# Grouped mixture of experts: the first five blocks run while rows are still being placed, and the shared units stand between the one-hot products

## The reference

```python
E, I, K = 64, 176, 6                                   # experts, width, chosen per token
probs = softmax(x @ gate_w.T)
topk_w, topk_idx = top_k(probs, K)
topk_w = topk_w / sum(topk_w)
h = silu(einsum('th,eih->tei', x, experts_w1))
y = einsum('tei,ehi->teh', h, experts_w2)
routed_out = einsum('teh,te->th', y, combine)          # combine holds topk_w at the chosen experts
g, u = split(x @ shared_gate_up.T, 2)
shared_out = silu(g) * u @ shared_down.T               # runs for every token
return routed_out + shared_out
```

## Time and profile before

| | us |
|---|---|
| median of 3 runs | 2220.29 |
| lowest and highest | 2219.08, 2224.95 |
| span of the profiled execution | 2224.5 |
| placement, first to last issue | 1301.4 to 1366.2 |
| first `turn` of the blocks | 1377.6 |
| last `down` of the blocks | 1598 |

### The profile page before, as it was taken

How to read it: one execution, slowest core, us unless ns; L and a number is a source line. 1 busy time by engine, 2 the same in 40 slices (tenths; PEclk the granted TensorE clock), 3 DMA queues, 4 the chain that set the end, 5 groups by cost and what they waited for, 6 DMA issues and landing times. The chain is left out here.

```text
span 2224.5 us, 43127 instructions
## 1 busy us (share of the span) xinstructions
PE 1997.6 (90%) x13031; PEld 1713.8 (77%) x13031; DVE 1498.0 (67%) x4236; ACT 1156.4 (52%) x2628; POOL 681.9 (31%) x1298
## 2 busy tenths in 40 slices
PE   5688796999999995799999884999879999987998
PEld 3444475779999992599999773999769999976887
DVE  6578576847787884788888771422278888875665
ACT  3656442847676661466666411444346666653333
POOL 3312201103334321233333155544323333312221
PEclk9889898999999996899999887999989999988999
DMA  2066502012122104430000023999820000014331
GB/s 66 9 115 154 169 18 71 1 48 79 52 78 71 58 20 155 159 110 0 0 0 0 28 92 117 316 315 318 271 81 16 21 21 14 14 31 121 116 112 41
DMA packets 145258, 193.66 MB, mean 87 GB/s; under 512 B 45084, under 2 KB 113285, under 8 KB 142217
## 3 DMA queue, kind: packets, MB, share of 16 engines
q1 hardware_dynamic: 121096, 153.51, 23.0%
q0 software_dynamic: 7632, 20.85, 2.5%
q10 hardware_dynamic: 16400, 17.70, 2.4%
HBM read 169.86 MB, written 56.62 MB: 102 GB/s over the span
## 5 line engine op out<-in xcount | busy, mean ns | idle before, releaser
L2613 DVE COPY l2f_x_t<-bank 128x256 f32<-128x256 f32 x111 | 47.1, 425 | 152.4 <-PE bank L2336 149.4
L2478 POOL DMA_INDIRECT l2f_y_rows<-l2f_y,l2f_target x111 | 112.0, 1009 | 121.8 <-ACT l2f_y L2446 119.4
L724 ACT ACTIVATE l1a_prob<-l1a_masked,l1a_shift,l1a_q_scale 128x512 f32<-128x512 f32 x128 | 104.5, 817 | 76.4 <-DVE l1a_shift L782 74.7
L724 ACT ACTIVATE l2a_prob<-l2a_masked,l2a_shift 128x512 f32<-128x512 f32 x128 | 92.7, 725 | 79.0 <-DVE l2a_shift L786 76.2
L724 ACT ACTIVATE l3a_prob<-l3a_masked,l3a_shift 128x512 f32<-128x512 f32 x128 | 92.7, 725 | 78.1 <-DVE l3a_shift L786 75.2
L2348 PE MATMUL bank<-l2f_x_t,l2f_w 128*128 128x128 f32 x888 | 117.4, 275 | 0.4 <-DVE l2f_x_t L2613 0.4
L1297 ACT ACTIVATE l0a_prob_t<-bank 128x512 f32<-128x512 f32 x128 | 76.2, 599 | 64.8 <-PE bank L1235 64.0
L2348 PEld LDWEIGHTS bank<-l2f_x_t,l2f_w 128*128 128x128 f32 x888 | 108.0, 192 | 0.7 <-issue 0.6
L1314 DVE TENSOR_REDUCE l0a_coarse<-bank 128x32 f32<-128x512 f32 x128 | 87.5, 688 | 26.5 <-PE bank L1225 24.7
L776 DVE CUSTOM_DVE_ANT_0 l3a_masked<-bank,l3a_side 128x512 f32<-128x512 f32 x128 | 88.4, 691 | 14.2 <-issue 12.9
L776 DVE CUSTOM_DVE_ANT_0 l2a_masked<-bank,l2a_side 128x512 f32<-128x512 f32 x128 | 88.4, 691 | 12.6 <-issue 10.8
(11 more groups left out here) (603 smaller groups left out, 7467.7 us busy)
## 6 DMA issues: line engine op xcount, KB each, us to landing
l2f_w<-w_rows SPq DMA_DIRECT2D x111, 304.0 KB
l1a_side<-rms SPq DMA_DIRECT2D x16, 1024.0 KB, 4.8
l2f_x_rows_of<-x_slots ACTq DMA_DIRECT2D x111, 128.0 KB
w_rows<-in_l2f_w SPq DMA_DIRECT2D x4, 2048.0 KB
l2f_hots<-l2f_y_rows SPq DMA_DIRECT2D x8, 768.0 KB, 10.0
l3f_raw<-in_l3f_w SPq DMA_DIRECT2D x24, 256.0 KB, 3.8
l3f_mix<-shares SPq DMA_DIRECT2D x16, 384.0 KB, 3.7
l2f_w_rest<-in_l2f_w SPq DMA_DIRECT2D x111, 48.0 KB
```

The lines of the kernel that those rows point to most:

```text
L724: act.activation(prob[:, unit, :], masked[:, unit, :], ACT.Exp, bias=shift[:, unit:unit + 1], scale=q_scale[:, slot, t:t + 1] if qk_norm e ...
L2478: pool.indirect_dma_start(y_rows, bass.IndirectOffsetOnAxis(target[:, b:b + 1], 0), y[:, b % of.Y_SLOTS, :], None).then_inc(y_stored[b % o ...
L2613: dve.tensor_copy(x_t[:, b % 2, :], turn_bank[b % 2][:, 0:D]).then_inc(x_kept, 1)
```

## The change

1. `x_placed` becomes six semaphores, one for each choice, and POOL places choice 5 of all eight tiles first, then choice 4, down to choice 0. Because a token's slots fall with the choice and every expert that has rows has at least one block, block b can hold only rows of choices 5 down to 5-b. So block b below 5 is complete when `x_placed[5-b]` is.
2. SP, not ACT, issues the row loads of blocks 0 to 10. Its order is: weights of blocks 0 to 5; rows of blocks 0 to 4, each behind its choice; weights of blocks 6 to 10; the wait for choice 0; rows of blocks 5 to 10; weights of block 11 and on. ACT issues rows from block 11 on.
3. PE runs blocks 0 to 4 one after the other (`turn`, `up`, `down` of a block with nothing between) and starts its pipelined order at block 5.
4. The first halves of units 6 to 11 and `shared_out(0)`, `shared_out(1)` stand between the 48 one-hot products on PE; DVE does their additions and products six one-hot pairs later. Only `shared_out(2)` and `shared_out(3)` are left behind the products.

```diff
+    AHEAD = CHOSEN - 1
+    SHARED_LAG = 6
+    shared_out_at = {1: 0, 3: 1}
+    shared_in_at = {8 + 5 * n: of.EARLY * of.SHARED + n for n in range(shared_units - of.EARLY * of.SHARED)}
...
+        x_placed = [st.sem(f"x_placed{k}") for k in range(chosen)]
...
+        def load_rows(engine, b):
+            wait_for(engine, x_turned, b - of.X_SLOTS + 1)
+            engine.dma_start(x_rows_of[:, b % of.X_SLOTS, :], x_slots[b * P:(b + 1) * P, :]).then_inc(x_loaded[b % of.X_SLOTS], 16)
...
-                for b in range(blocks):
+                for b in range(of.W_SLOTS):
+                    load_weights(b)
+                for b in range(of.AHEAD):
+                    sp.wait_ge(x_placed[chosen - 1 - b], 16 * TT)
+                    load_rows(sp, b)
+                for b in range(of.W_SLOTS, of.W_SLOTS + of.AHEAD):
+                    load_weights(b)
+                sp.wait_ge(x_placed[0], 16 * TT)
+                for b in range(of.AHEAD, of.AHEAD + of.X_SLOTS):
+                    load_rows(sp, b)
+                for b in range(of.W_SLOTS + of.AHEAD, blocks):
                     load_weights(b)
...
                         last = pe.matmul(place_bank[:, 0:blocks], in_block[:, n, :], of_block[:, n, :],
                                          start=(n == 0), stop=(n == TT * chosen - 1))
+                        if n in shared_in_at:
+                            shared_in(shared_in_at[n])
+                        if n in shared_out_at:
+                            shared_out(shared_out_at[n])
                 last.then_inc(targets_ready, 1)
-                shared_out(0)
-                shared_out(1)
-                for pair in range(of.EARLY, pairs):
-                    shared_in(pair)
                 for pair in range(of.EARLY, pairs):
                     shared_out(pair)
                 pe.wait_ge(pair_kept, shared_units)
                 pe.wait_ge(added, TT)
-                turn(0)
-                turn(1)
-                up(0)
-                for b in range(blocks):
+                for b in range(of.AHEAD):
+                    turn(b)
+                    up(b)
+                    down(b)
+                turn(of.AHEAD)
+                turn(of.AHEAD + 1)
+                up(of.AHEAD)
+                for b in range(of.AHEAD, blocks):
...
-                act.wait_ge(x_placed, 16 * TT * chosen)
-                for b in range(of.X_SLOTS):
-                    load_rows(b)
...
-                        if b + of.X_SLOTS < blocks:
-                            load_rows(b + of.X_SLOTS)
+                        if b >= of.AHEAD and b + of.X_SLOTS < blocks:
+                            load_rows(act, b + of.X_SLOTS)
...
-                for t in range(TT):
-                    for k in range(chosen):
+                for k in reversed(range(chosen)):
+                    for t in range(TT):
                         pool.indirect_dma_start(x_slots, bass.IndirectOffsetOnAxis(slot_i[:, t, k:k + 1], 0), m.x_n[:, t, :],
-                                                None).then_inc(x_placed, 16)
+                                                None).then_inc(x_placed[k], 16)
...
+                    if n - of.SHARED_LAG in shared_out_at:
+                        add_shared(shared_out_at[n - of.SHARED_LAG])
+                    if n - of.SHARED_LAG in shared_in_at:
+                        shared_multiply(shared_in_at[n - of.SHARED_LAG])
```

More of the change, by code:

```diff
@@ L2250, in grouped_mixture @@
         (loaded, shared_loaded, own, logits_ready, shifted, exp_done, masked, places_ready, owner_done, owner_turned,
[L2251 removed]
+         owner_kept, counters_set, one_hots, targets_ready, targets_kept, pair_ready, pair_kept, shared_h_done,
          shared_y_ready) = st.sems(
             "loaded", "shared_loaded", "own", "logits_ready", "shifted", "exp_done", "masked", "places_ready", "owner_done",
[L2254 removed]
+            "owner_turned", "owner_kept", "counters_set", "one_hots", "targets_ready", "targets_kept", "pair_ready",
             "pair_kept", "shared_h_done", "shared_y_ready")
@@ L2308, in logits, with shared_in @@
                     last.then_inc(logits_ready, 1)
[L2310 to L2320, removed]
+                def shared_in(n):
+                    pair, u = n // of.SHARED, n % of.SHARED
+                    wait_for(pe, pair_kept, n - 1)
+                    bank = pair_bank[n % 2]
+                    for up in range(2):
+                        first = (2 * D + P) * up
+                        for c in range(DC):
+                            last = pe.matmul(bank[:, up * 2 * P:(up + 1) * 2 * P], shared_w[:, u, first + c * P:first + (c + 1) * P],
+                                             m.x_t[:, c, pair * 2 * P:(pair + 1) * 2 * P], start=(c == 0), stop=(c == DC - 1))
+                    last.then_inc(pair_ready, 1)
                 def shared_out(pair):
@@ L2361, in _ @@
                 pe.wait_ge(shared_loaded, 16)
-                shared_in(0)
+                for n in range(of.SHARED):
+                    shared_in(n)
                 pe.wait_ge(masked, 1)
@@ L2370, in _ @@
                 last.then_inc(places_ready, 1)
-                shared_in(1)
+                for n in range(of.SHARED, 2 * of.SHARED):
+                    shared_in(n)
                 pe.wait_ge(owner_done, 1)
@@ L2557, in _, with add_shared, shared_multiply @@
                 dve.tensor_copy(part[:], part_i[:]).then_inc(part_done, 1)
+                def add_shared(pair):
+                    for n in range(2):
+                        t = 2 * pair + n
+                        dve.wait_ge(shared_y_ready, t + 1)
+                        dve.tensor_tensor(m.x[:, t, :], m.x[:, t, :], y_bank[n][:, 0:D], ALU.add).then_inc(added, 1)
+                def shared_multiply(n):
+                    pair, u = n // of.SHARED, n % of.SHARED
+                    dve.wait_ge(pair_kept, n + 1)
+                    dve.wait_ge(shared_y_ready, 2 * (pair - 1))
+                    dve.tensor_tensor(shared_h[:, pair % 2, u, :], shared_gate[:, n % 2, :], shared_up[:, n % 2, :],
+                                      ALU.mult).then_inc(shared_h_done, 1)
                 dve.wait_ge(part_done, 1)
@@ L2585, in _ @@
                 dve.scalar_tensor_tensor(target[:], place_bank[:, 0:blocks], -1.0, empty[:], ALU.add, ALU.add).then_inc(targets_kept, 1)
[L2586 to L2589, removed]
                 for pair in range(of.EARLY, pairs):
```

3 lines of the change are left out of this document (removed).

## The result

| | before | changed |
|---|---|---|
| median, us | 2222.32 (4 runs) | 2209.41 (4 runs) |
| lowest and highest | 2219.08, 2224.95 | 2207.44, 2211.42 |
| span of the profiled execution | 2224.5 | 2205.7 |

The ratio is 0.9947 with a 95% interval of 0.9934 to 0.9961: 11.8 us faster (8.7 to 14.7), where 14.0 was forecast. The two profiled spans differ by more, 18.8 us. That is no contradiction. The first placement, before which nothing was changed, starts at 1301.41 in the one trace and at 1299.18 in the other, and in all traces of this study anywhere from 1296.6 to 1306.9.

A forecast was written before the change was run, and what follows sets the result against it. PE, busy 1997.6 of 2224.5 us, was the bound, so only its waits or work leaving the end's path could gain. 17.3 - 1.3 - 2.0 = 14.0 us; 2220.3 - 14.0 = 2206.3 us, range 2202 to 2222.

The forecast's parts named there:

- The mechanism and its size: Blocks 0 to 4 leave the end's path; block 5 turned at 1370.1 instead of 1387.4, a first gain of 17.3 us.
- The lone blocks: Blocks 0 to 4 run singly on PE, 3.8 us each, from about 1346 to 1365.
- POOL's pace: Placements on POOL slow beside DVE's spread one-hot work; 1.3 us lost, from about 1 us gained to 3.5 lost.
- Landing of the last choice: POOL issues its last placement by 1365.24, as before; choice 0's rows land at about 1367.5.
- SP's queue: SP issues weights of blocks 6 to 10 by 1366.8, 0.7 us before block 5's rows are placed at 1367.5.
- The clock: First blocks of the pipelined order run at a lower clock after PE's wait; 2.0 us lost, between 0 and 3.4.
- The base: First profile of the kernel before: block 0 turned at 1377.6, block 5 at 1387.4, the point to beat.
- The signs I had named: Block 5's turn at 1370 to 1375, lone blocks within 1346 to 1368, prompt ACT, last placement 1366 to 1369, 1.96 us blocks.
- A: PE's "done" signals come late in blocks 0 to 4 too; block 5 7.0 us later than before, 2227 us; chance 0.20.
- B: Half clock in blocks 0 to 4, 6.3 us each, eats most of the gain; 4 us left, 2216 us; chance 0.15.
- C: No gain for another reason, such as row loads behind weights on SP landing 10 us late; 2219 us; chance 0.05.

The follow-up runs named there:

- ahead_two: The changed kernel with two early blocks (run before the pipelined order) instead of five; ratio to before 0.9972, median 2211.88 us.
- before_again: The unchanged kernel from before, run and profiled a second time with no edit; ratio to before 0.9994, profiled span 2223.2 us.
- sp_late: The changed kernel with SP issuing weights of blocks 6 to 8 behind rows of blocks 2 to 4, weights 9 and 10 behind rows 5 to 10; ratio 0.9944.
- after_again: The changed kernel run and profiled again with no edit, ten later runs; ratio to before 0.9963, 8.2 us faster, median 2208.82 us.
- warm: The changed kernel with unused matmuls filling PE's waits behind block 3 (14) and block 4 (26); ratio to before 0.9956.
- sp_late_again: A repeat, without edit, of sp_late; ratio to before 0.9937, median 2207.93 us.
- sp_late_fill: sp_late plus unused matmuls on PE behind block 3 (12) and block 4 (16); ratio to before 0.9955.
- early_only: The changed kernel's early blocks, placing by choice and SP row loads, but shared units left behind the one-hot products as before; ratio to before 0.9967.

## Why the prediction was right, point by point

**The mechanism and its size.** Five blocks left the end's path. From block to block pass 1.98 us, not 1.96: I divided by 110 though the first two turns start together. That is 9.9 us for five; ahead_two shows 3.8 for two.

**The lone blocks.** Forecast 3.8 us and `turn(0)` at P + 45; measured 3.6 and P + 36. The products ended 9 us earlier than worked out (P + 30.4 against P + 39.2), because five queued one-hot products pass PE in 1.1 us, 0.22 each: the 0.45 us that I read was DVE's pace, and DVE works ahead while PE has a shared unit. So what is put between them is not simply added, as I had it. It cost nothing either way.

**POOL's pace: wrong in sign.** I took +1.3 us between bounds of -1 and +3.5; it was -2.5 to -3.4 against before_again, outside them. My lower bound of 1 us did not follow from my own rows: 14 placements at 0.27 us each are 3.8 us that DVE's work can cost, and 3.2 of them came back (21.8 against 18.6). The traces show that POOL is slow where DVE's one-hot work is dense and fast where shared work stands between. The Trainium skill (SBUF — State Buffer, "Who interferes with whom") states that where VectorE and GpSimd contend, whichever issues first has the shared port pair for a whole instruction. Read as in the prediction, as a count of instructions, it would have made the term nothing, nearer than my 1.3 but not the gain that was measured.

**Landing of the last choice.** I took 2.3 us from POOL's last issue to the landing; it was 4.0, because the weights of blocks 6 to 10 are under way then: in sp_late, without them, it is 2.4. I had named SP's queue as the one to watch, but for its issue time, not for the transfers behind it. The issue time came in as well, in after_again, where the wait for block 4 made the row loads 1.2 us late.

**The clock.** 2.0 us at the first pipelined blocks, as taken from between 0 and 3.4: warm has 7.8 instead of 9.9 us there. But the kernel before pays it too in its usual execution (turn(0) to turn(10) in 20.5 us, 17.8 in the first profile), so it was no cost of the change.

**The base.** The first profile held 5.5 us of late signals that other executions lack. With before_again as the base block 5 stands at P + 68.0 + 9.9 = 77.9, and my steps put it at 1370.1 - 1301.4 = P + 68.7: 9.2 us, less 1.3 for POOL, 7.9, with nothing for the clock, since both kernels pay it. Measured were 11.6: 7.9, plus 4.2 for POOL (placing ended at P + 61.9, where I had 66.1), less 1.3 for landing and row load (5.2 us, where I had 3.9), plus 0.7 because the low clock cost before_again 2.7 us and the changed kernel 2.0; the sum is 11.5. So the forecast of 14.0 came near 11.6 because a base that was 8.1 us too late made up for a POOL that I had made 4.2 us too slow and for a clock term of 2.0 that should not have been there. The direction and the 9.9 us of the five blocks were reasoned; the closeness of the total is luck, and against the 8.2 us of the ten later runs 14.0 is not close.

**The signs I had named.** Block 5 was turned at P + 67.1 (69.3 in after_again), forecast P + 68.6 to 73.6. POOL was through with its last placement at P + 61.9, ahead of the forecast of P + 64.6 to 67.6. The lone blocks began 8 us before their window. ACT took the units promptly, and the blocks after came at 1.98 us.

**Rivals.** A did not happen: in nine traces with early blocks no wait of that kind stood in them. B happened in part of the executions, after_again among them, and goes with a loss of 2.4 us, not 10, nearly all of it through SP's queue. C did not happen as priced (10 us); weights beside the last placements cost 1.6 us of landing.

## What to carry to other kernels

Before a stall without a named releaser becomes a term of the sum, look at a second execution, and count from an event that the change cannot move. When work is moved between two busy engines, ask a third that shares something with one of them: here the thinned DVE work was worth 3 us on POOL. And on a queue that issues both early and urgent transfers, the early ones cost twice, by their issue slots and waits (1.2 us in after_again) and by the bytes under way when the urgent one must land (1.6 us here).

## What the runs showed of the hardware that I had not expected

- The place of a stage in the span moves by 10 us (1296.6 to 1306.9) between executions of programs that are alike up to there. Much of the scatter of the timed runs may be this: those of sp_late_again fall into two groups, 2204.4 to 2205.0 and 2210.8 to 2211.3, and its profiled run (2211.27) differs from that of sp_late (2206.34) by 4.9 us in P and by less than 0.1 us behind it.
- ACT waited 6 to 15 us for PE's units 9 to 11 in one execution of twelve; in the others it waited 1.08 us where the units follow each other and 2.2 us where one-hot products stand between them.
- Where PE had the low clock for 6.8 us around the first shared matmuls, it lost the full clock again 34 us later in the middle of lone blocks (after_again, warm, ahead_two, sp_late_fill); where it had it for 3.4 us, it kept it for 51 us (the changed kernel's profile, sp_late, sp_late_again), over the same instructions. It is no rule: early_only had it for 6.8 us as well and kept the full clock for 58 us. With two small matmuls in each gap of 0.5 us it was kept too, in the one execution that tried it.
